# Placing 64 index gathers between the scatters of one GpSimd queue in a two-layer graph kernel

## The reference

```python
h = max(layernorm(x), 0)
msg = h[src] * edge_weight[:, None]                       # layer 0
x = x + segment_sum(msg, dst) @ W_neigh + b_neigh + h @ W_self.T
# layer 1, on the rows grouped by src
seg_sum, seg_max, seg_mean = of edge_attr over src        # 32 columns each
u = concat(seg_sum, where(cnt > 0, seg_max, 0), seg_mean, u[0])
x = x + relu(u @ W1 + b1) @ W2 + b2
```

## Time and profile before

| what | value |
|---|---|
| median of 3 timed runs | 1600.9 us (1599.28 to 1601.22) |
| profiled execution, its span | 1898.8 us |
| its own time outside of the span | not recorded |
| POOL busy in the span | 1125.6 us (59%) |
| DVE busy in the span | 1274.2 us (67%) |
| PE busy in the span | 1004.9 us (53%) |

### The profile page before, as it was taken

The page is one execution under the profiler, slowest core; times in us unless marked ns, Lnnn a source line. Parts: engine busy times, 40 slices in busy tenths (PEclk is TensorE's granted clock), DMA queues, the critical chain, the costliest instruction groups (busy, mean ns, idle before and its releaser), DMA issues. The chain is left out here.

```text
span 1898.8 us, 39252 instructions
## 1 busy us (share of the span) xinstructions
PE 1004.9 (53%) x13560; PEld 866.0 (46%) x13561; DVE 1274.2 (67%) x3119; ACT 743.8 (39%) x1962; POOL 1125.6 (59%) x1212
## 2 busy tenths in 40 slices
PE   1022445444444446432433332243599999999996
PEld 1011344443334435322323331242488888888885
DVE  3033667666656667544686664596699998999985
ACT  1001456555545556422222211132155554545553
POOL 7755445445464445466776676765066666666663
PEclk9975666666666666655555555566599999999997
DMA  9910133333333334322434442344399999999997
GB/s 283 167 21 11 43 76 83 77 78 77 76 66 76 79 77 93 75 62 70 120 99 105 111 109 73 77 114 111 98 207 221 222 215 205 214 213 222 210 210 95
DMA packets 521162, 229.67 MB, mean 121 GB/s; under 512 B 486253, under 2 KB 493677, under 8 KB 520285
## 3 DMA queue, kind: packets, MB, share of 16 engines
q0 software_dynamic: 162672, 98.52, 30.1%
q1 hardware_dynamic: 334606, 111.32, 28.1%
q10 hardware_dynamic: 23680, 17.25, 3.6%
HBM read 138.46 MB, written 88.33 MB: 119 GB/s over the span
## 5 line engine op out<-in xcount | busy, mean ns | idle before, releaser
L930 POOL DMA_INDIRECT by_win<-rows,idx_win x391 | 382.3, 978 | 355.7 <-DVE idx_win L366 233.9
L923 POOL DMA_INDIRECT xg_all<-in_x_dram,src_i x390 | 394.1, 1011 | 161.9 <-issue 117.0
L1308 PE MATMUL ps<-ident,h 128*128 128x128 f32 x588 | 142.9, 390 | 322.6 <-issue 115.0
L1481 POOL DMA_DIRECT2D out_dram<-rows x97 | 156.5, 1613 | 167.7 <-ACT rows L1655 167.7
L1308 PEld LDWEIGHTS ps<-ident,h 128*128 128x128 f32 x588 | 96.2, 200 | 343.5 <-issue 123.6
L1396 ACT ACTIVATE sq<-xc 128x512 f32<-128x512 f32 x147 | 92.5, 629 | 406.8 <-DVE xc L1040 270.9
L1321 PE MATMUL ps<-wsT,hT 128*128 128x128 f32 x784 | 167.7, 385 | 152.1 <-DVE arena L1090 93.3
L1321 PEld LDWEIGHTS ps<-wsT,hT 128*128 128x128 f32 x784 | 156.3, 295 | 157.2 <-issue 154.6
L1414 ACT ACTIVATE h<-xc,stat 128x64 f32<-128x64 f32 x784 | 196.3, 333 | 0.0
L482 ACT ACTIVATE hist<-ps 32x256 f32<-32x256 f32 x196 | 72.6, 371 | 246.9 <-remote 228.5
L1610 PE MATMUL ps<-w_sb,arena 128*96 128x64 f32 x1568 | 157.8, 254 | 8.8 <-issue 6.0
(11 more groups left out here) (204 smaller groups left out, 2567.7 us busy)
## 6 DMA issues: line engine op xcount, KB each, us to landing
rows<-flag_d POOLq DMA_DIRECT2D x98, 288.0 KB, 8.7
out_dram<-rows POOLq DMA_DIRECT2D x97, 256.0 KB, 9.3
rows<-message SPq DMA_DIRECT2D x588, 36.4 KB, 4.7
message<-m_row SPq DMA_DIRECT2D x48, 388.0 KB
arena<-in_x_dram SPq DMA_DIRECT2D x70, 256.0 KB
out_dram<-arena SPq DMA_DIRECT2D x70, 256.0 KB
rows<-slot_d POOLq DMA_DIRECT2D x98, 144.0 KB, 6.2
by_win<-zeros ACTq DMA_DIRECT2D x12, 808.5 KB
```

The costliest lines, as they stand in the source:

```text
L923: nc.gpsimd.indirect_dma_start(out=xg[g % RX][:, t % GT, :], out_offset=None, in_=x, in_offset=bass.IndirectOffsetOnAxis(ap=(src_i[:, t:t ...
L930: nc.gpsimd.indirect_dma_start(out=by_win, out_offset=bass.IndirectOffsetOnAxis(ap=idx_win[0:parts, t:t + 1], axis=0), in_=rows[0:parts, t ...
L1308: last = nc.tensor.transpose(hT_of[n % 2][:, P * k:P * k + P], h[n % 2][:, 2 * k:2 * k + 2, :].rearrange("p a c -> p (a c)"), ident[:, :])
L1481: pool.dma_start(nodes_of(out, g), y[b][:, :, :], accum_op=ALU.add).then_inc(summed_out[b], 16)
```

## The change

The gathers of groups 0 to 7 leave the start of GpSimd's program. They stand before the scatters of groups 8, 13, 18, 23, 28, 33, 38 and 43. The one wait for all 14 attribute loads is split in three: the first load before column 0, the next three before column 32, the others before column 128. To keep within the number of semaphores, the loads of edge weights and next destinations share one, and the two stores of start tables share one.

```diff
-        loaded = {n: sem(f"loaded_{n}") for n in ("weights", "src", "edges", "weight", "next", "attr", "starts", "counts")}
+        loaded = {n: sem(f"loaded_{n}") for n in ("weights", "src", "edges", "later", "attr", "starts", "counts")}
...
-        starts_out, counts_out = sem("starts_out"), sem("counts_out")
+        starts_out = sem("starts_out")
...
+        attr_first, attr_second = sem("attr_first"), sem("attr_second")
...
+        GATHER_AT = [EARLY + 5 * n for n in range(EARLY)]
...
-                    sp.dma_start(rows[:, t:t + n, 0:DE], attr_pt[:, t:t + n, :]).then_inc(loaded["attr"], 16)
+                    which = attr_first if t == 0 else attr_second if t <= 3 * step_t else loaded["attr"]
+                    sp.dma_start(rows[:, t:t + n, 0:DE], attr_pt[:, t:t + n, :]).then_inc(which, 16)
...
-                edge_load(sp, ew, weight, "weight")
+                edge_load(sp, ew, weight, "later")
...
-                sp.wait_ge(starts_out, 16)
+                sp.wait_ge(starts_out, 32)
...
                 pool.wait_ge(loaded["src"], 16)
-                for g in range(EARLY):
-                    gather(g)
                 pool.wait_ge(zeroed, 16 * ZC)
-                pool.wait_ge(loaded["attr"], 16 * (-(-FT // (4 * GT)) + 1))
                 pool.wait_ge(made["rows"], 1)
                 for t in range(FT + 1):
+                    if t == 0:
+                        pool.wait_ge(attr_first, 16)
+                    if t == 4 * GT:
+                        pool.wait_ge(attr_second, 16 * 3)
+                    if t == 16 * GT:
+                        pool.wait_ge(loaded["attr"], 16 * (-(-FT // (4 * GT)) - 3))
                     if t % GT == 0:
+                        if t // GT in GATHER_AT:
+                            gather(GATHER_AT.index(t // GT))
                         pool.wait_ge(r_win["idx"], t // GT + 1)
                     scatter(t)
...
-                dve.wait_ge(loaded["next"], 16 * 2)
+                dve.wait_ge(loaded["later"], 16 * 4)
...
-                dve.wait_ge(loaded["weight"], 16 * 2)
```

More of the change, by code:

```diff
@@ L785, in _ @@
                     n = min(step_t, FT - t)
-                    sp.dma_start(rows[:, t:t + n, 0:DE], attr_pt[:, t:t + n, :]).then_inc(loaded["attr"], 16)
+                    which = attr_first if t == 0 else attr_second if t <= 3 * step_t else loaded["attr"]
+                    sp.dma_start(rows[:, t:t + n, 0:DE], attr_pt[:, t:t + n, :]).then_inc(which, 16)
                 sp.dma_start(rows[0:TAIL, FT, 0:DE], attr[FT * P:E, :]).then_inc(loaded["attr"], 16)
-                edge_load(sp, ew, weight, "weight")
-                sp.dma_start(next_i[:, 0:FT], dst[1:FT * P + 1].rearrange("(p t) -> p t", p=P)).then_inc(loaded["next"], 16)
+                edge_load(sp, ew, weight, "later")
+                sp.dma_start(next_i[:, 0:FT], dst[1:FT * P + 1].rearrange("(p t) -> p t", p=P)).then_inc(loaded["later"], 16)
                 sp.dma_start(next_i[0:TAIL - 1, FT:FT + 1],
-                             dst[FT * P + 1:E].rearrange("(p o) -> p o", o=1)).then_inc(loaded["next"], 16)
+                             dst[FT * P + 1:E].rearrange("(p o) -> p o", o=1)).then_inc(loaded["later"], 16)
                 for table in (message[E:ROWS, :], message[ROWS + E:2 * ROWS, :]):
@@ L844, in _ @@
                 sp.wait_ge(made["counts"], 1)
-                sp.dma_start(starts_d[1, :].rearrange("(p l) -> p l", p=DIGIT), start_i["win"][:, :]).then_inc(counts_out, 16)
-                sp.wait_ge(counts_out, 16)
+                sp.dma_start(starts_d[1, :].rearrange("(p l) -> p l", p=DIGIT), start_i["win"][:, :]).then_inc(starts_out, 16)
+                sp.wait_ge(starts_out, 16)
                 for n in range(NB):
```

## The result

Three timed runs of the changed kernel have a median of 1626.3 us (1622.83 to 1627.62); with the median of 1600.9 us before it, the ratio is 1.015 [1.011, 1.020]. It is slower by 25.4 us, clear of the noise though under 2%, where the prediction had 26. The predicted time was 1627.

What follows compares the result with a forecast made beforehand. POOL's queue of indirect DMAs was taken as the bound. First scatter earlier (-52.6), 64 gathers paid later (+81.1 + 4) and waits filled (-7) gave +26, so 1627 us; own range 1612 to 1639, 8 in 10 1572 to 1645.

Steps and rivals of the forecast that it cites:

- the stated +26: Whole kernel: first scatter earlier (-52.6), gathers paid later (+81.1 + 4), some waits filled (-7), so 1627 us.
- remainder: Kernel before: timed median less POOL's work without waits, 22.4 us, the most that POOL's waits could be.
- The sum of POOL's chain: Kernel before, start to end: POOL's indirect DMAs without waits, VectorE's trail and the rest add up to 1578.5 us.
- lower bound: Low end of the forecast's own range: first scatter at 32 and 22 us of waits filled, given as +11.
- The filled waits (-7 us): Between the scatters: moved gathers fill POOL's waits for indices, a third of the 22 us, so 7 come free.
- The attribute loads: POOL's start: first load lands at 38 to 39 us and holds the first scatter; later split waits cost nothing.
- the 298 us: Profiled 1898.8 us against timed 1600.9: excess put down mostly to PE's late releases under the profiler.
- Waits less by some 80: Profile of the changed kernel: POOL's waits for indices fall below 233.9 us by some 80.
- the pair of signs: Profiled span may shrink while timed runs grow, which would prove that the waits belong to the profiled execution.
- the first rival: Ranking bounds timed runs too, so gathers fit into 233.9 us of waits: 1548 to 1601 us, chance 0.25.
- The third rival: Late releases at the start are real, group 1's indices come at 115 us: 1660 to 1682 us, chance 0.08.

Runs made afterwards that it cites:

- three groups first: Changed kernel with gathers of groups 0 to 2 back at the start: 1596.7 us, 0.999 on P; 1.005 and 1.002 on L, against the kernel before.
- one wait: Changed kernel with all three attribute waits put before column 0: 1.029 and 1.035 on L, 1.041 on M, against the kernel before.

## Why the prediction was right, and where it wasn't

The mechanism held: on chip P POOL's chain of indirect DMAs is the bound, and gathers taken out of the start and put between scatters are paid there. That the time came within 1 us is luck. Three sets have the change at +25.4, +17.3 and +21.1 us, the first is the nearest to the forecast, and the stated +26 rests on a share of a remainder that no run shows.

**The sum of POOL's chain: right, piece by piece.** I set the predicted pieces beside those of the changed kernel's timeline:

| piece | predicted | measured |
|---|---|---|
| first scatter at | 39.0 | 40.2 |
| 391 scatters and 64 gathers | 501.6 + 85.1 = 586.7 | 631.94 - 40.20 = 591.7 |
| 327 gathers | 431.6 | 435.4, to 1067.3 |
| VectorE's trail to the last message | 13 | 14.2, to 1081.5 |
| the rest | 540.7 | 539.6 |
| sum | 1611.0 | 1621.1 |

(The last message's store goes out at 1079.09 and needs 2.4 us to land, the median of its line.) The prediction counts the landing twice, though: its 540.7 us start at the issue of the store, 1358.09, so the 2 us of landing are in them already. Like for like, from issue to end, it is 542.0 us in the changed kernel. Its sum for the kernel before should be 1576.5 and the remainder 24.4; the difference of 26 us isn't touched. Its lower bound is a slip too: a first scatter at 32 with 22 us filled makes +3.5, so 1604, and not +11, which is the case of 39 with 22 filled. Two of the pieces come from these lists of POOL's groups in the changed kernel, from 39 to 631.9 us and on to 1067.5:

```profile
L933 POOL DMA_INDIRECT by_win<-rows,idx_win x391 | 389.5, 996 | 149.6 <-issue 118.3 <-DVE idx_win L366 31.4
L926 POOL DMA_INDIRECT xg_all<-in_x_dram,src_i x64 | 63.6, 993 | 19.5 <-issue 19.5
```

```profile
L926 POOL DMA_INDIRECT xg_all<-in_x_dram,src_i x326 | 335.0, 1027 | 99.4 <-issue 99.4
```

The scatters took 996 ns and not 978, which is 7.2 us. VectorE is now busy beside them nearly all the time, but the chip is another one too, and no run tells the two apart. The gathers took 993, between the 963 and 1020 of the earlier trace rows. The page *DMA: Bandwidth & Descriptors* of the Trainium skill, under "SWDGE vs HWDGE vs iDMA", says that GpSimd builds the descriptors in a part of on-chip memory from which VectorE locks it out while it works in its 2-port mode. If that is the reason, which no run here shows, it costs 18 ns of 978 here, no more.

**The remainder of 22.4 us: half of it found.** The sum falls 10.1 us short of the span. Time outside of the span is 1.7, and the median of the timed runs lies 3.5 above the profiled one. That makes 15.3, where the prediction had left 22.4 - 7 = 15.4. The two agree because the forecast of the time did; it is no second proof. What stands in the place of the remainder is now known: 10.1 us of pieces longer than assumed, 1.7 outside of the span, and 3.5 from one run to the next.

**The filled waits (-7 us): not measured.** The changed kernel has 0.7 us of waits for indices behind its first scatter. How many the kernel before has on P no trace shows. A bound comes from the run with three groups first on P. Its lengths with 91.6 as the first scatter make 91.6 + 510.4 + 432.0 + 549.5 = 1583.5 us (391 scatters, 389.1 busy and 121.3 of issue gaps; the tail from 607.20 to 1039.24; the rest to 1588.7), and with 1.7 outside of the span and 6.3 (its own median over its profiled time) 1591.5, 9 under the 1600.9. So 7 is possible, and anything from 0 to 9 as well. The two repeats in which the change cost 17.3 and 21.1 us speak for the upper end or above it, but their intervals hold 6 to 35.

**The attribute loads: right.** First landing at 39 to 40, the split waits at columns 32 and 128 at nothing. What the split is worth when gathers don't fill the start is seen in one wait: 79.2 to 79.6 us for the first scatter.

**Where the 298 us are from: wrong.** The prediction said, "I take that for mostly an effect of the profiled execution, since the sum leaves it 22 us in a timed one." The second half holds, the first fell with the first repeat of the kernel before. The profile first shown and the times first shown were from executions in which PE's releases behave differently, the profile like chip M (1898.0), the times like P (1600.9). The conclusion was saved because it didn't rest on the cause: the sum of what POOL does came within 22 us of the timed median, and that left no place for the waits, whatever made them.

**"Waits less by some 80" and the pair of signs: wrong as a rule.** The span did fall while the timed runs rose, but for another reason, the other kind of chip; so the "proof of the reading" came out and proved nothing. Where the comparison is a fair one (one wait, on L and M), the waits for indices were 242.0 and 240.8 us, against 246.0 and 230.6 in the kernel before. That also corrects the first rival. It took 234 us of waits for room. On a chip where releases are late the ranking does set POOL's pace, and still there is hardly any room: with 64 gathers added between the scatters the ranking itself ends 50.3 us later on L and 62.8 on M. That each gather holds PE's releases back is the reading of this, and not shown gather by gather. The third rival (indices of group 1 at 115 us) erred in the same way: with POOL silent at the start they come at 33.5 us, on M as on P, and the lateness moves with the gathers. By that arithmetic the changed kernel itself should cost 83 - 52 = about +31 us on L or M; from one wait, less its 40 us of later start, it is 20 to 31. Both are estimates. It wasn't run there.

**Open.** Why some chips release PE's waiters late while POOL issues indirect DMAs, and some don't. Three chips can't tell whether it is the chip or something that lasted as long as a set, though both sets on L were alike, and both on P. No kernel here beats the one before on P beyond the measurement: by its sum POOL works there nearly without a break from 10 us on until the second block, and three groups first merely uses the same time in another order.

## What to carry to other kernels

Before waits are counted as room, add up the suspected engine's own work without any wait, and hold it against the timed median, not the span: where the two nearly agree, the waits aren't in the timed runs and moved work is paid in full. Work that stands in an idle start is nearly free up to the landing of the first thing that is waited for (24 gathers here, 31 us of work, put the first scatter off by 3.1 us); more delays the chain, less leaves it idle. And time the kernel before anew in every set of runs: here it alone differed by 20% between chips, over ten times what the change did.

## What the runs showed of the hardware

- On chips L and M 62 to 64% of PE's releases came over 1 us late (or are missing in the trace) in the kernel before, up to POOL's last gather, and none behind it; on P 1 to 2% in every kernel profiled there. The kernel before is 297 to 331 us longer on L and M than on P. It goes with POOL's issuing of indirect DMAs, not with the amount of DMA traffic (11 against 77 instructions on VectorE in the same 39 us at the same DMA share).
- An indirect DMA of 128 rows holds POOL for 0.96 to 1.03 us (means of the groups shown) and an issue gap of 0.30, whether it scatters or gathers. The page *Perfetto Trace Analysis* of the Trainium skill, under "DMA Instruction — SWDGE (GPSIMD)", says that such a slice ends when the descriptors are written, not when the data has moved. A chain that is set by the number of DMAs agrees with it: on P 24 of them moved cost 25.4 us.
- The time of a run was its span and 1.7 to 1.8 us, the profiled execution's too (1926.0 against 1924.2, 1590.4 against 1588.7).
